# The last stage of layer 0 and the first of layer 1 made one in a two-layer attention kernel over a graph

## The chip, the cores and the metric

The kernel runs on one core of a Trainium2 chip. The time is the device time of one execution, in microseconds (us). The kernel before took 3869.91 us, the median of three runs (3863.47, 3869.91, 3873.05). Its profiled execution took 3871.49 us, with a span of 3869.6 us from the first to the last instruction.

## The reference

There are 3125 nodes with 64 features, and 100,000 edges from `src` to `dst`. A first part (`_L0_gnn_ref`) sends messages along the edges, sums them by node and runs three residual blocks; a layernorm follows. The part that matters here is two attention convolutions one after the other, each with two heads of 64:

```python
q = (x @ wq + bq).reshape(n, H, C)
k = (x @ wk + bk).reshape(n, H, C)
v = (x @ wv + bv).reshape(n, H, C)
alpha = jnp.einsum('ehc,ehc->eh', q[dst], k[src]) / jnp.sqrt(C)
amax = jax.ops.segment_max(alpha, dst, num_segments=n)
ex = jnp.exp(alpha - amax[dst])
a = ex / (denom[dst] + 1e-16)                 # denom: segment_sum(ex, dst)
out = jax.ops.segment_sum(a[:, :, None] * v[src], dst, num_segments=n)
return out.mean(axis=1) + x @ ws + bs
```

`x` of the second convolution is the result of the first. The sum of both and the residual goes through a last layernorm.

## The kernel before

The kernel computes the attention densely. A table of 3125 sources by 3136 targets holds how many edges each pair has; its logarithm is added to the scores, so that pairs without an edge vanish in the exponential. Sources are cut into NT = 25 tiles of 125, targets into CH = 7 chunks of D = 448. A score tile is 125 sources by 2 heads by 448 targets, in float32.

The first two thirds of the span (to about 2660 us) count the edges and do the first part of the model. The change does not touch them. Then come the two attention layers, `l` = 0 and 1. Each begins with projections: for each chunk a K and a Q matmul (L1101), which VectorE (DVE) and ScalarE (ACT) copy out (L874, L589), then V for 25 source tiles (L1106, copied with its bias at L879). Then come eight stages, `c` = 0 to 7. Stage `c` does two things at once:

- the scores of chunk `c`: TensorE (PE) multiplies (`scores`, L1121), DVE adds the logarithms (`score`, L898) and keeps a running maximum (`running`, L910);
- the weighted sums of chunk `c` - 1: GpSimd (POOL) subtracts the maximum of each target (L445), ACT takes the exponential (`exps`, L602), PE multiplies with V (`weighted`, L1144) and with ones for the denominators (L1153).

Stage 0 has only scores, stage 7 only weighted sums. In stage 7 DVE has no scores and takes 15 of the 25 subtractions (`by_vector`, L925). A stage ends when the maximum is known: PE transposes it (`move_max`, L1127), DVE reduces it (L916), PE spreads it over all partitions (`spread_max`, L1133), ACT copies it to `max_of_targets` (`spread`, L597). Only then can POOL begin on that chunk.

After the weighted sums of a chunk the denominators are copied (`copy_sums`), spread (L1159), copied again (`copy_spread`, L612) and inverted by DVE (`invert`, L931); POOL multiplies (`normalize`, L438) and PE projects (`project`, L1167 and L1168 in layer 0). ACT's `next_h` (L616) writes that chunk of layer 1's input. This happens one stage later, in the middle of it, for chunks 0 to 5; for chunk 6 it stands at the end of the layer, and layer 1's projections begin behind it.

Each engine runs its own list of instructions in the written order, and waits on semaphores. A matmul that writes a bank of the accumulation memory (`PS`) waits until the bank has been copied out. Scores alternate between banks 0, 1 and banks 2, 3; sums and denominators hold banks 4 and 5, the running maximum 6 and 7.

Of the kernel before, what the change touches and what calls it, by code (L numbers as in the profile page):

```python
# [7 lines left out]
F = 64  # L8
R = 16
P = 125  # L10
NT = N // P
# [11 lines left out]
CH = 7  # L23
LOADS = 2 * 7 + 2
BLK = 4
MW = 112
# [9 lines left out]
PP = PART + LEAD  # L36
INVERT = 11
# [3 lines left out]
assert SLOTS == NT + LEAD  # L41
# [20 lines left out]
def build(nc, x, src, dst, edge_attr, W_att, W_i, b_i, W_j, b_j, W_v, b_v, rd_W, rd_b, rr_W, rr_b, gate,  # L62
# [17 lines left out]
    with ctx:  # L80
# [153 lines left out]
        def by_vector(c, i):  # L234

            return c == CH - 1 and i % QN in (1, 3, 4)

        shifts = {}
        for v in range(2):
            n = 0  # L240
            for l in range(2):
                for c in range(CH):
                    for i in range(NT):
                        n += by_vector(c, i) == v
                        if by_vector(c, i) == v:
                            shifts[l, c, i] = n
# [6 lines left out]
        part_bank = 2 * (PP % 2)  # L253

        def slot_of(i):

            return (i + (i >= PP)) % 2
# [114 lines left out]
        def _(pool):  # L372
# [61 lines left out]
            for l in range(2):  # L434
                def normalize(c):
                    pool.wait_ge(sem("sums_out"), 2 * (l * CH + c + 1))
                    pool.wait_ge(sem("sums_inverted"), 2 * (l * CH + c + 1))
                    nc.gpsimd.tensor_tensor(AOn, AOn, DN, ALU.mult).then_inc(sem("normalized"), 1)  # L438

                for c in range(CH):  # L440
                    pool.wait_ge(sem("max_spread"), l * CH + c + 1)
                    for i in range(NT):
                        if not by_vector(c, i):
                            t = Ts[:, (l * ATT + c * NT + i) % SLOTS]
                            nc.gpsimd.tensor_tensor(t, t, MB, ALU.subtract).then_inc(sem("shifted"), 1)  # L445
                        if c and i == INVERT + 3:
                            normalize(c - 1)
                normalize(CH - 1)
# [3 lines left out]
        def _(act):  # L452
# [131 lines left out]
            for l in range(2):  # L584

                act.wait_ge(sem("bias_scaled"), 1)
                for c in range(CH):
                    act.wait_ge(sem("qk_in_psum"), 2 * (CH * l + c) + 2)
                    nc.scalar.activation(qT[:, c * D:(c + 1) * D], qk_bank(2 * c + 1), ACT.Identity, scale=0.125, bias=BC[:, 12 + l:13 + l]  # L589
                                         ).then_inc(sem("q_copied"), 1)  # L590
# [628 lines left out]
```

## Time and profile before

| | us |
|---|---|
| median of three runs | 3869.91 |
| profiled execution | 3871.49 |
| its span | 3869.6 |
| maximum of layer 0's chunk 6 spread (stage 7 can begin) | 3242.69 |
| layer 0's last projection begins | 3291.06 |
| first K and Q matmul of layer 1 | 3295.22 |
| first V matmul of layer 1 | 3316.29 |
| first scores of layer 1 | 3327.87 |
| maximum of layer 1's chunk 0 spread | 3388.84 |

Times are us from the start of the span. The two moments at which a maximum is spread are the start of ACT's copy plus its duration: 3241.77 + 0.92 and 3387.92 + 0.92. Between them lies the stretch that the change rewrites, 146.15 us. In rows of a timeline the first number is the start, the second the duration; several like instructions are merged, with "xN" their count. A float32 matmul shows as two records. PEclk is the granted TensorE clock as a share of 2.4 GHz: 1.00 is 2.4 GHz, 0.50 is 1.2 GHz.

### The profile page before, as it was taken

The page shows a single profiled execution, that of the slowest core. Times are in us where ns is not written, and L with a number is a line of the kernel's source. Part 1 is how long each engine was busy: PE and PEld are TensorE (multiplying, and loading weights), DVE is VectorE, ACT ScalarE, POOL GpSimd, SP SyncE. Part 2 cuts the span into 40 slices and gives each one's busy share as a digit, 9 for nine tenths or more (in the row PEclk, how much of TensorE's full clock was granted, in tenths as well). Part 3 has the DMA queues.
Part 4 walks back from the last instruction along what each step waited for, and adds up shares of the span by engine and source line. Part 5 has one row for each costly group of instructions (what it writes and reads, how often), then busy time and mean ns, then how long its engine had stood idle before and what let it go on. Part 6 is the DMA issues. An engine that isn't in the chain of part 4 may idle for free.

```text
span 3869.6 us, 56741 instructions
## 1 busy us (share of the span) xinstructions
PE 3063.6 (79%) x18659; PEld 1701.0 (44%) x18659; DVE 2706.2 (70%) x8606; ACT 669.4 (17%) x868; POOL 2811.3 (73%) x1917
## 2 busy tenths in 40 slices
PE   4787778777777877787778777876788888799996
PEld 3555555555555555555555555543222222322222
DVE  4666666666666666666666666656888888678786
ACT  2000000000000000000000000014343444043343
POOL 3588888888888888888888888872576776088684
PEclk7988898889889988988898889888799999699998
DMA  8411111111111111111111111113544452223330
GB/s 310 152 13 13 12 13 13 12 13 13 13 12 13 13 13 12 13 13 13 12 13 13 13 13 13 13 7 71 162 140 128 134 145 71 58 77 87 76 77 9
DMA packets 244257, 194.37 MB, mean 50 GB/s; under 512 B 146300, under 2 KB 224981, under 8 KB 244181
## 3 DMA queue, kind: packets, MB, share of 16 engines
q1 hardware_dynamic: 86035, 159.92, 13.9%
q0 software_dynamic: 137984, 26.19, 11.9%
q10 hardware_dynamic: 20162, 7.27, 0.9%
q8 instruction: 46, 0.75, 0.1%
q14 instruction: 30, 0.25, 0.0%
HBM read 112.79 MB, written 80.42 MB: 50 GB/s over the span
## 4 chain that ended last, share of the span: by engine, by line
DMA 28%; PE 20%; issue 19%; POOL 19%; DVE 9%; ACT 2%; SPq 2%; POOLq 1%; DVEq 0%; ACTq 0%
DMA edge_counts<-small 27%; POOL nodes_and_gaps L397 10%; POOL edge_counts L406 8%; PE PS L1121 7%; PE PS L1144 6%; PE PS L1153 3%; DVE counts_and_logs L886 2%; DVE scores L898 2%; DVE PS L910 2%; SPq L329 2%; DVE scores L925 1%; PE PS L1101 1%; PE PS L1133 1%; DMA edge_counts<-counts_and_logs 1%; PE PS L1127 0%
## 5 line engine op out<-in xcount | busy, mean ns | idle before, releaser
L1037 PE MATMUL PS<-scores 128*128 128x320 bf16 x11760 | 1839.8, 321 | 537.5 <-DVE scores L765 537.5
L1037 PEld LDWEIGHTS PS<-scores 128*128 128x128 bf16 x11760 | 1222.7, 105 | 1166.6 <-DVE scores L765 546.7
L406 POOL DMA_INDIRECT edge_counts<-small x752 | 1208.2, 1607 | 264.8 <-issue 264.8
L397 POOL DMA_INDIRECT nodes_and_gaps<-xj_rows,small x784 | 800.1, 1021 | 289.7 <-issue 129.2
L445 POOL TENSOR_TENSOR scores<-scores,max_of_targets 125x896 f32<-125x896 f32 x320 | 730.0, 2321 | 382.4 <-ACT max_of_targets L597 382.4
L726 DVE SCALAR_TENSOR_TENSOR scores<-PS,small,scores 128x256 bf16<-128x256 f32 x784 | 332.8, 480 | 666.6 <-PE PS L1017 666.5
L765 DVE TENSOR_SCALAR scores<-scores,small 128x192 bf16<-128x192 bf16 x3920 | 745.2, 296 | 3.5
L898 DVE TENSOR_TENSOR scores<-PS,counts_and_logs 125x896 f32<-125x896 f32 x350 | 377.5, 1082 | 146.7 <-PE PS L1153 61.1
L1121 PE MATMUL PS<-q_features,k_features 64*125 64x448 f32 x1400 | 383.6, 632 | 108.5 <-DVE scores L898 104.9
L602 ACT ACTIVATE scores<-scores 125x896 f32<-125x896 f32 x350 | 328.4, 948 | 360.2 <-POOL scores L445 346.6
L1144 PE MATMUL PS<-scores,v_nodes 125*64 125x448 f32 x1400 | 352.2, 591 | 20.3 <-ACT scores L602 20.3
L910 DVE TENSOR_TENSOR PS<-PS,scores 125x896 f32<-125x896 f32 x322 | 350.5, 1089 | 0.0
L739 DVE TENSOR_SCALAR scores<-scores,small 128x632 bf16<-128x632 f16 x784 | 281.9, 419 | 0.0
L1121 PEld LDWEIGHTS PS<-q_features,k_features 64*125 64x125 f32 x1400 | 113.4, 196 | 376.0 <-DVE scores L898 272.9
L521 ACT ACTIVATE scores<-nodes_and_gaps 128x512 bf16<-128x512 f32 x98 | 61.7, 630 | 1134.7 <-DVE nodes_and_gaps L748 1134.7
L516 ACT ACTIVATE scores<-PS 128x128 f32<-128x128 f32 x98 | 27.1, 277 | 1091.0 <-PE PS L1024 1091.0
L1153 PE MATMUL PS<-scores,dense_weights 125*32 125x448 f32 x1400 | 184.3, 575 | 0.0
L1144 PEld LDWEIGHTS PS<-scores,v_nodes 125*64 125x64 f32 x1400 | 74.1, 139 | 250.5 <-issue 149.9
L748 DVE TENSOR_TENSOR nodes_and_gaps<-nodes_and_gaps,PS 128x512 f32<-128x512 f32 x98 | 67.3, 687 | 114.6 <-DMA nodes_and_gaps<-xj_rows,small 114.2
L1016 PE MATMUL PS<-identity_scaled,keys 128*128 128x128 f16 x784 | 109.3, 220 | 15.0 <-ACT q_features L479 7.8
L1017 PE MATMUL PS<-identity,keys 128*128 128x128 f16 x784 | 109.4, 220 | 0.0
L886 DVE SCALAR_TENSOR_TENSOR counts_and_logs<-counts_and_logs 125x2240 f32<-125x2240 f32 x35 | 106.9, 3054 | 0.0
(162 smaller groups left out, 1714.9 us busy)
## 6 DMA issues: line engine op xcount, KB each, us to landing
counts_and_logs<-edge_counts SPq DMA_DIRECT2D x70, 980.0 KB
edge_counts<-counts_and_logs SPq DMA_DIRECT2D x50, 766.0 KB
edge_counts<-counts_and_logs SPq DMA_DIRECT2D x35, 980.0 KB
nodes_and_gaps<-xj_rows,small POOLq DMA_INDIRECT x784, 2.5
edge_counts<-small POOLq DMA_INDIRECT x752
counts_and_logs<-edge_counts SPq DMA_DIRECT2D x70, 113.8 KB
scores<-in_edge_attr_dram ACTq DMA_DIRECT2D x95, 48.0 KB
edge_counts<-counts_and_logs SPq DMA_DIRECT2D x35, 113.8 KB
```

The lines of the kernel that those rows point to most:

```text
L397: pool.indirect_dma_start(gx[u][:, s * F:(s + 1) * F], None, xj_dram, bass.IndirectOffsetOnAxis(ap=dcur[u][:, s:s + 1], axis=0)).then_inc( ...
L406: pool.indirect_dma_start(cnt_dram, bass.IndirectOffsetOnAxis(ap=index[:, s:s + 1], axis=0), value[:, s:s + 1], None, compute_op=ALU.add). ...
L445: nc.gpsimd.tensor_tensor(t, t, MB, ALU.subtract).then_inc(sem("shifted"), 1)
L602: nc.scalar.activation(t, t, ACT.Exp).then_inc(sem("weighed"), 1)
L726: nc.vector.scalar_tensor_tensor(ranked[:, s, :], PS[:, 5, 2 * EP * pair:2 * EP * pair + 2 * EP], keyc[:, s:s + 1], lowh[:, EP * (1 - e):E ...
L765: nc.vector.tensor_scalar(spread[:, s, :, k, :], pieces[:, :, s * F:(s + 1) * F], hi_is[:, k, s:s + 1], None, ALU.mult).then_inc(sem("tile ...
L898: nc.vector.tensor_tensor(Ts[:, n % SLOTS], score_slot[slot_of(i)], C5[k % CBUFS][:, i % QN].unsqueeze(1).to_broadcast([P, HEADS, D]), ALU ...
L910: nc.vector.tensor_tensor(RM if i == NT - 1 else RP, RP, Ts[:, n % SLOTS], ALU.max).then_inc(sem("max_run"), 1)
L1037: ins = nc.tensor.matmul(PS[:, b, 0:HI * F], onehot[:, s, b * P:b * P + 128], spread[:, s, i].rearrange("p h f -> p (h f)"), start=first a ...
L1121: ins = nc.tensor.matmul(score_slot[slot_of(i)][:, h, :], kT[q, i * P:(i + 1) * P], qT[q, c * D:(c + 1) * D], start=True, stop=True)
L1144: nc.tensor.matmul(AO[F * h:F * h + F, :], V[:, i, h, :], Ts[:, n % SLOTS, h, :], start=i == 0, stop=i == NT - 1, skip_group_check=True)
L1153: ins = nc.tensor.matmul(DEN[32 * g:32 * g + 32, :], ones, Ts[:, (n - i + e) % SLOTS, h, :], start=e < 2, stop=e >= NT - 2, skip_group_che ...
```

## The change

The stages are numbered `g` = 0 to 14 through both layers. Stage 7 of layer 0 and stage 0 of layer 1 become one, `g` = JOIN = 7, written out in a function of its own on PE, and layer 1's projections are spread over it:

- While the weighted sums of layer 0's chunk 6 run, PE does K and Q of layer 1 for chunk 0 to 4 behind weighted tile 0 to 4, projects chunk 5 of layer 0 behind tile 5 (before: behind tile 16), and does K and Q of chunk 5 behind tile 7.
- From weighted tile 8 on, a score tile of layer 1 stands behind each weighted tile (JLEAD = -8), 17 of them by the last weighted tile. Then come scores 17 to 20 with V of layer 1 between them, the projection of chunk 6, K and Q of chunk 6, and scores 21 to 24.
- All 25 subtractions of that stage go to POOL; `by_vector` holds only for the last stage of layer 1.
- V is copied out by ACT instead of DVE (an activation can't add a row of biases), so each V matmul is followed by a matmul that contracts over one row and adds the bias (`next_v`).
- Divisions of chunk 5 stand at the start of the stage on DVE, and POOL normalizes chunk 5 behind its third subtraction.

```diff
+LAST = 2 * CH - 1
+JOIN = CH
+JLEAD = -8
+JPP = 21
+JPART = 5
+EARLY = 17
-        def by_vector(c, i):
-            return c == CH - 1 and i % QN in (1, 3, 4)
+        def by_vector(g, i):
+            return g == LAST and i % QN in (1, 3, 4)
...
+                    if g == JOIN - 1 and i == 2 or projects(g + 1) is not None and i == INVERT + 3:
+                        normalize(g - 1)
+                if g == JOIN - 1:
+                    normalize(g)
...
+            def copy_v(b):
+                n = min(4, NT - 4 * b)
+                act.wait_ge(sem("v_in_psum"), 7 + b + 1)
+                nc.scalar.activation(V[:, 4 * b:4 * b + n].rearrange("p t h c -> p t (h c)"),
+                                     PS[0:P, 4 + b % 2, 0:n * 128].rearrange("p (t c) -> p t c", t=n), ACT.Copy).then_inc(sem("v_copied"), 1)
...
+                    if g == JOIN:
+                        if 1 <= i <= CH - 2:
+                            copy_q(1, i - 1, PS[:, 2 * ((i - 1) % 2) + 1, 0:D])
+                        if i == JPART + 1:
+                            next_h(CH - 2)
+                        if i == JPART + 3:
+                            copy_q(1, CH - 2, PS[:, 3, 0:D])
+                        if i == JPART + 5:
+                            begin_max(g)
...
+                if g == JOIN:
+                    for part in range(2):
+                        invert(g - 2, part)
+                    for c in range(CH - 1):
+                        copy_k(1, c, PS[:, 2 * (1 if c == CH - 2 else c % 2), 0:D])
+                    for i in range(EARLY + 2):
+                        score_and_run(g, i)
+                    for part in range(2):
+                        invert(g - 1, part)
+                    for i in range(EARLY + 2, JPP):
+                        score_and_run(g, i)
+                    copy_k(1, CH - 1, PS[:, 2, 0:D])
...
+            def next_qk(c, r):
+                pe.wait_ge(sem("attended"), c + 1)
+                for j, w in enumerate((wk_(1), wq_(1))):
+                    nc.tensor.matmul(PS[:, 2 * r + j, 0:D], w, h_(1, c * D, D), start=True, stop=True).then_inc(sem("qk_in_psum"), 1)
+
+            def next_v(b):
+                if b >= 2:
+                    pe.wait_ge(sem("v_copied"), 7 + b - 1)
+                for t in range(4 * b, min(4 * b + 4, NT)):
+                    to = PS[0:P, 4 + b % 2, t % 4 * 128:(t % 4 + 1) * 128]
+                    nc.tensor.matmul(to, h_(1, t * P, P), wv_(1), start=True, stop=False)
+                    ins = nc.tensor.matmul(to, ones[0:1, 0:1].to_broadcast([1, P]), BR[0:1, 128:256], start=False, stop=True)
+                ins.then_inc(sem("v_in_psum"), 1)
...
+            def join(g):
+
+                pe.wait_ge(sem("scored"), g * NT)
+                for i in range(NT):
+                    weighted(g - 1, i)
+                    if i < CH - 2:
+                        if i >= 2:
+                            pe.wait_ge(sem("k_copied"), CH + i - 1)
+                            pe.wait_ge(sem("q_copied"), CH + i - 1)
+                        next_qk(i, i % 2)
+                    if i == JPART:
+                        pe.wait_ge(sem("k_copied"), CH + CH - 3)
+                        project(g - 2)
+                    if i == JPART + 2:
+                        pe.wait_ge(sem("q_copied"), CH + CH - 3)
+                        next_qk(CH - 2, 1)
+                    if i + JLEAD >= 0:
+                        if i + JLEAD == 0:
+                            pe.wait_ge(sem("k_copied"), CH + CH - 1)
+                            pe.wait_ge(sem("q_copied"), CH + CH - 1)
+                        scores(g, i + JLEAD)
+                scores(g, EARLY)
+                spread_sums(g - 1)
+                scores(g, EARLY + 1)
+                pe.wait_ge(sem("spread_copied"), g)
+                next_v(0)
+                next_v(1)
+                scores(g, EARLY + 2)
+                next_v(2)
+                next_v(3)
+                scores(g, EARLY + 3)
+                next_v(4)
+                pe.wait_ge(sem("scored"), g * NT + JPP - 1)
+                project(g - 1)
+                next_qk(CH - 1, 1)
...
+                scores(g, JPP)
+                scores(g, JPP + 1)
+                next_v(5)
+                scores(g, JPP + 2)
+                next_v(6)
+                scores(g, JPP + 3)
+                move_max(g)
+                spread_max(g)
```

PE at the start of stage 7, in the list of the kernel before. L1133 spreads the maximum of chunk 6, L1159 the denominators of chunk 5; L1144 are weighted sums and L1153 denominators.

```order
L1127 MATMUL PS<-identity,running_max 112x125 x8
L1144 MATMUL PS<-scores,v_nodes 64x448 x2
L1153 MATMUL PS<-scores,dense_weights 32x448 x2
L1133 MATMUL PS<-identity,small 125x112 x8
L1159 MATMUL PS<-dense_weights 128x448
L1144 MATMUL PS<-scores,v_nodes 64x448 x4
L1153 MATMUL PS<-scores,dense_weights 32x448 x4
```

The same place in the changed kernel, whose line numbers are its own: L1209 are weighted sums, L1218 denominators, and L1165 is K and Q of layer 1.

```order
L1224 MATMUL PS<-dense_weights 128x448
L1209 MATMUL PS<-scores,v_nodes 64x448 x2
L1165 MATMUL PS<-h_features,layer_weights 128x448 x2
L1209 MATMUL PS<-scores,v_nodes 64x448 x2
L1218 MATMUL PS<-scores,dense_weights 32x448 x4
L1165 MATMUL PS<-h_features,layer_weights 128x448 x2
L1209 MATMUL PS<-scores,v_nodes 64x448 x2
L1165 MATMUL PS<-h_features,layer_weights 128x448 x2
```

K and Q moved from behind the layer to between the first weighted tiles.

PE from the end of stage 7 to the end of layer 1's stage 0, before: L1167 and L1168 project chunk 6, L1101 is K and Q, L1106 is V, L1121 are scores.

```order
L1144 MATMUL PS<-scores,v_nodes 64x448 x2
L1153 MATMUL PS<-scores,dense_weights 32x448 x2
L1159 MATMUL PS<-dense_weights 128x448
L1167 MATMUL PS<-dense_weights 64x448
L1168 MATMUL PS<-h_features,layer_weights 64x448
L1101 MATMUL PS<-h_features,layer_weights 128x448 x14
L1106 MATMUL PS<-layer_weights,h_features 125x128 x25
L1121 MATMUL PS<-q_features,k_features 125x448 x50
L1127 MATMUL PS<-identity,running_max 112x125 x8
```

In the changed kernel, from the last weighted tile: L1186 are scores, L1172 is V and L1173 its bias.

```order
L1186 MATMUL PS<-q_features,k_features 125x448 x2
L1209 MATMUL PS<-scores,v_nodes 64x448 x2
L1218 MATMUL PS<-scores,dense_weights 32x448 x2
L1186 MATMUL PS<-q_features,k_features 125x448 x4
L1224 MATMUL PS<-dense_weights 128x448
L1186 MATMUL PS<-q_features,k_features 125x448 x2
L1172 MATMUL PS<-layer_weights,h_features 125x128
L1173 MATMUL PS<-bias_rows,dense_weights 125x128
```

Further on, where V's tile 19 is followed by the projection of chunk 6 (L1230, L1231):

```order
L1172 MATMUL PS<-layer_weights,h_features 125x128
L1173 MATMUL PS<-bias_rows,dense_weights 125x128
L1230 MATMUL PS<-dense_weights 64x448
L1231 MATMUL PS<-h_features,layer_weights 64x448
L1165 MATMUL PS<-h_features,layer_weights 128x448 x2
L1186 MATMUL PS<-q_features,k_features 125x448 x4
L1172 MATMUL PS<-layer_weights,h_features 125x128
L1173 MATMUL PS<-bias_rows,dense_weights 125x128
```

V now stands behind score tile 18, in pairs with its bias, and the projection of chunk 6 behind score tile 20, where before all 50 score matmuls stood behind both.

## Rows read from the trace of the kernel before

**Rows 1.** The page, busy time of each engine in the span

```profile
PE 3063.6 (79%) x18659; PEld 1701.0 (44%) x18659; DVE 2706.2 (70%) x8606; ACT 669.4 (17%) x868; POOL 2811.3 (73%) x1917
```

**Rows 2.** Windows (us, busy us of PE, PEld, DVE, ACT, POOL; clock; DMA), stages

```profile
3242.00:3289.00 47.00, 38.92 (x208) 9.02 (x206) 38.69 (x19) 26.13 (x31) 30.91 (x11) 0.93 0.00 1
3289.00:3328.00 39.00, 35.51 (x84) 20.82 (x84) 10.06 (x16) 5.06 (x8) 1.13 (x1) 0.52 0.00 0
3328.00:3388.00 60.00, 38.05 (x126) 14.58 (x128) 50.66 (x51) 1.00 (x2) 0.00 (x0) 0.76 0.36 94
3388.00:3456.00 68.00, 63.27 (x326) 18.02 (x326) 51.67 (x51) 26.90 (x30) 51.35 (x25) 0.97 0.32 83
```

**Rows 3.** Timeline (start, us, engine, line, what), ACT

```profile
3241.77 0.92 ACT L597 ACTIVATE max_of_targets<-PS 125x896 f32<-125x896 f32 x1 [0.85 <-PE PS L1133]
...
3294.54 0.63 ACT L616 ACTIVATE h_features<-PS,bias_columns 64x448 f32<-64x448 f32 x1 [7.80 <-PE PS L1168]
...
3387.92 0.92 ACT L597 ACTIVATE max_of_targets<-PS 125x896 f32<-125x896 f32 x1 [56.01 <-PE PS L1133]
```

**Rows 4.** Timeline, PE, weighted sums at the start of stage 7

```profile
3246.78 3.25 PE L1144 MATMUL PS<-scores,v_nodes 125*64 125x448 f32 x8 [4.27 <-ACT scores L602]
3249.96 1.72 PE L1153 MATMUL PS<-scores,dense_weights 125*32 125x448 f32 x8
3251.61 2.22 PE L1144 MATMUL PS<-scores,v_nodes 125*64 125x448 f32 x8
```

**Rows 5.** Windows of PE alone (us, busy us; clock; DMA), K, Q, V of both layers

```profile
3295.00:3316.40 21.40, 21.18 (x29) 0.50 0.00 0
3316.40:3327.20 10.80, 10.76 (x51) 0.50 0.00 0
2667.30:2678.00 10.70, 10.67 (x29) 1.00 0.66 156
2678.00:2684.20 6.20, 6.09 (x51) 1.00 1.05 253
```

**Rows 6.** Timeline, PE, projections of chunk 5 and chunk 6

```profile
3271.16 0.92 PE L1167 MATMUL PS<-dense_weights 128*64 128x448 f32 x2
...
3272.90 0.97 PE L1144 MATMUL PS<-scores,v_nodes 125*64 125x448 f32 x4
...
3291.06 1.75 PE L1167 MATMUL PS<-dense_weights 128*64 128x448 f32 x2 [4.90 <-POOL dense_weights L438]
```

**Rows 7.** The page, the exponentials

```profile
L602 ACT ACTIVATE scores<-scores 125x896 f32<-125x896 f32 x350 | 328.4, 948 | 360.2 <-POOL scores L445 346.6
```

**Rows 8.** Timeline, POOL

```profile
3289.88 1.13 POOL L438 TENSOR_TENSOR dense_weights<-dense_weights 128x448 f32<-128x448 f32 x1 [13.65 <-DVE dense_weights L931]
3388.92 51.35 POOL L445 TENSOR_TENSOR scores<-scores,max_of_targets 125x896 f32<-125x896 f32 x25 [97.91 <-ACT max_of_targets L597]
```

**Rows 9.** Timeline, PE, a pair of tiles in layer 1's stage 1

```profile
3400.85 1.02 PE L1121 MATMUL PS<-q_features,k_features 64*125 64x448 f32 x4
3401.80 0.97 PE L1144 MATMUL PS<-scores,v_nodes 125*64 125x448 f32 x4
...
3404.56 0.96 PE L1153 MATMUL PS<-scores,dense_weights 125*32 125x448 f32 x8
3405.45 1.02 PE L1121 MATMUL PS<-q_features,k_features 64*125 64x448 f32 x4
```

**Rows 10.** Timeline, DVE: two divisions, and the last tiles of layer 1's stage 0

```profile
3286.78 2.96 DVE L931 RECIPROCAL dense_weights<-dense_weights 128x224 f32<-128x224 f32 x2 [7.58 <-ACT dense_weights L612]
...
3377.43 1.08 DVE L898 TENSOR_TENSOR scores<-PS,counts_and_logs 125x896 f32<-125x896 f32 x1
3378.43 1.09 DVE L910 TENSOR_TENSOR PS<-PS,scores 125x896 f32<-125x896 f32 x1
3379.62 1.09 DVE L910 TENSOR_TENSOR running_max<-PS,scores 125x896 f32<-125x896 f32 x1
```

**Rows 11.** Windows of all engines, inside layer 1's stage 0

```profile
3336.00:3338.00 2.00, 1.02 (x8) 0.29 (x4) 2.00 (x3) 0.00 (x0) 0.00 (x0) 1.00 0.00 0
3342.00:3344.00 2.00, 1.86 (x6) 0.50 (x4) 2.00 (x3) 0.00 (x0) 0.00 (x0) 0.50 0.29 61
```

More of the change, by code:

```diff
@@ L962, in _ @@
+            for part in range(2):
+                invert(LAST, part)
+            outputs(CH - 1)
             dve.wait_ge(sem("attended"), 2 * CH)
@@ new lines, in scores @@
+            def scores(g, i):
+                n = g * NT + i
+                pause = pause_of(g)
+                if n >= 2:
+                    pe.wait_ge(sem("scored"), n if i == pause else n - 2 if i == pause + 1 else n - 1)
+                if i == pause + 1 and projects(g) is not None:
+                    pe.wait_ge(sem("attended"), g - 1)
+                c = g % CH
+                for h in range(HEADS):
+                    q = slice(F * h, F * h + F)
+                    ins = nc.tensor.matmul(score_slot[slot_of(g, i)][:, h, :], kT[q, i * P:(i + 1) * P], qT[q, c * D:(c + 1) * D], start=True, stop=True)
+                ins.then_inc(sem("scores_in_psum"), 1)
@@ new lines, in weighted @@
+            def weighted(g, i):
+                n = g * NT + i
+                pe.wait_ge(sem("weighed"), n + 1)
+                if i == 0 and g:
+                    pe.wait_ge(sem("sums_out"), 2 * g)
+                for h in range(HEADS):
+                    nc.tensor.matmul(AO[F * h:F * h + F, :], V[:, i, h, :], Ts[:, n % SLOTS, h, :],
+                                     start=i == 0, stop=i == NT - 1, skip_group_check=True)
+                if i % 2 == 0 and i < NT - 1:
+                    return
+                if i == 1 and g:
+                    pe.wait_ge(sem("spread_copied"), g)
+                for e in range(i - i % 2, i + 1):
+                    for h in range(HEADS):
+                        q = 2 * (e % 2) + h
+                        ins = nc.tensor.matmul(DEN[32 * q:32 * q + 32, :], ones, Ts[:, (n - i + e) % SLOTS, h, :],
+                                               start=e < 2, stop=e >= NT - 2, skip_group_check=True)
+                ins.then_inc(sem("weighted_sums"), 1 + i % 2)
@@ new lines, in _ @@
+            for g in range(2 * CH + 1):
+                if g == JOIN:
+                    join(g)
+                    continue
+                for i in range(LEAD):
+                    if g <= LAST:
+                        scores(g, i)
+                for i in range(NT):
+                    if g:
+                        weighted(g - 1, i)
+                    if projects(g) is not None and i == PART:
+                        pe.wait_ge(sem("scored"), min(2 * ATT, g * NT + PP - 1))
+                        project(g - 2)
+                    if g <= LAST and i + LEAD < NT:
+                        scores(g, i + LEAD)
+                    if g <= LAST and i == NT - 2:
+                        move_max(g)
+                if g <= LAST:
+                    spread_max(g)
+                if g:
+                    spread_sums(g - 1)
```

456 lines of the change are left out of this document (210 added, 246 removed).

## The prediction, on record before the changed kernel ran

> **What bounds the kernel now.** The page's busy shares come first, and they mislead: PE 79%, POOL 73%, DVE 70% are means over parts with different limits [rows 1]. So I read windows by stage next. The change rewrites one stretch, from the moment when layer 0's last maximum is spread, 3241.77 + 0.92 = 3242.69, to the moment when layer 1's first one is, 3387.92 + 0.92 = 3388.84 [rows 3]. That is 146.15 us, and nothing ahead of it or behind it changes its list. The stretch has three parts, each with another limit [rows 2]. Stage 7 of layer 0 (47 us): PE is 38.92 us busy and DVE 38.69. Projections (39 us): PE is busy for 35.51 us while DVE has 10, ACT 5, POOL 1, and the clock is 0.52. Stage 0 of layer 1 (60 us): DVE is busy for 50.66 us, POOL idle, PE at 38.05 with a clock of 0.76. The reader is to see that in each part other engines stand still, so laying the parts over each other can gain much, until one engine has the sum of the work. A mixed stage, for comparison, takes 68 us with PE at 63.27 and a clock of 0.97 [rows 2]: there PE is the limit.
>
> **Prices.** At the full clock (2.4 GHz) a score tile costs PE 0.95 us (3400.85 to 3401.80), the denominators of two tiles 0.89 (3404.56 to 3405.45), and two tiles in all 4.60 (3400.85 to 3405.45), so a weighted tile (4.60 - 1.90 - 0.89) / 2 = 0.90 [rows 9]. At 1.2 GHz two weighted tiles cost 3249.96 - 3246.78 = 3.18, so 1.6 each, and denominators 1.65 [rows 4]; a score tile 1.86 [rows 11]. K and Q of a chunk: 21.4 / 7 = 3.0 at the half clock, 10.7 / 7 = 1.53 at the full one; V: 10.8 / 25 = 0.43 or 6.2 / 25 = 0.25 a tile [rows 5]. A projection of layer 0: 3272.90 - 3271.16 = 1.74 full, 3294.54 - 3291.06 = 3.48 half [rows 3, 6]. POOL: 51.35 / 25 = 2.05 a subtraction beside DVE's scores, 1.13 a normalization [rows 8]. DVE: 1.0 from one operation to the next, so 2.0 a score tile [rows 10]. ACT: 0.95 an exponential [rows 7], 0.63 a copy of 448 columns [rows 3]; with a semaphore on each side I count 0.8 for a copy on which PE waits.
>
> The bias matmul that follows each V matmul has no row. It streams the same 128 columns; its price lies between nothing (if it runs beside V's, on other rows of the array) and that of a V matmul. I take the upper end, since columns seem to set the price: a K or Q matmul has 448 and costs 10.7 / 14 = 0.76, of which 128 / 448 is 0.22, near V's 0.25 [rows 5]. So four V tiles cost 2.0 us at full clock (between 1.0 and 2.0) and 3.45 at half.
>
> **The clock decides the sum.** K, Q and V of layer 1 kept PE busy for 31.94 of 32.2 us at 0.50 and never rose; the same instructions in layer 0 began at 1.00 and stayed there [rows 5]. These matmuls use 64 of the array's 128 rows. Weighted tiles, which use nearly all rows and columns, bring the clock back: at the start of stage 7 they cost the half-clock price until about 3251.6, five us after the first [rows 4]. Scores alone swing between 1.00, with PE busy half of the time, and 0.50 at 1.86 of 2.00 [rows 11]. So sparse matmuls seem to count for less.
>
> The Trainium skill, "TensorE: Matmul & The Clock Gate", section "Part 1: The HAM clock gate", says that the gate follows how busy PE has lately been, and that sustained matmuls release it. By that rule the joined stage, where PE hardly pauses, would run at 2.4 GHz to the end; it is the first rival below. The stretch of 32 us at 0.50 [rows 5] does not agree with busy time alone as the measure.
>
> **The sum, with t = 0 at 3242.69.**
>
> 1. K, Q and the first nine weighted tiles. PE's first weighted tile starts as before, at t = 3246.78 - 3242.69 = 4.1. Weighted tile 0, K and Q of chunk 0, tile 1 and the first denominators at half clock: 1.6 + 3.0 + 1.6 + 1.65 = 7.9, t = 12.0. Then the clock is full: seven weighted tiles 6.3, three denominators 2.7, five K and Q 7.7, the projection of chunk 5 1.7, together 18.4; and a wait for the last Q copy, 0.8: t = 31.2. POOL has exponential 8 ready by 9 x 2.05 + 1.13 + 0.95 = 20.5, so losing DVE's help in subtracting costs nothing: the 15 subtractions moved are hidden behind PE. The two divisions of chunk 5 (2.96, [rows 10]) are done before POOL's third subtraction.
> 2. Scores 0 to 16 among weighted tiles 9 to 24: 17 x 0.95 + 16 x 0.90 + 8.5 x 0.89 = 38.1, t = 69.3. DVE needs 2.0 a tile against PE's 2.3, POOL ends at 25 x 2.05 + 1.13 = 52.4. PE is the limit.
> 3. The tail. Score 17, the spread of denominators, score 18: 0.95 + 0.9 + 0.95, t = 72.1. ACT's copies end meanwhile. V 0 and 1: 4.0, t = 76.1. Score 19 and V 2: 3.0, t = 79.1. Here I let the clock fall, since half of each V pair contracts over 64 rows and the other half over one. V 3 3.45, score 20 1.86, V 4 3.45, t = 87.8. Divisions (2.96) and normalization (1.13) of chunk 6 start at about 74 on DVE, behind score 18, and end by 79: not late. Projection 3.5, copy 0.8, K and Q 3.0, copy 0.8: t = 95.9. Scores 21, 22, V 5, score 23, V 6, score 24: 4 x 1.86 + 3.45 + 0.86 = 11.8, t = 107.7. DVE: last score and two maxima 3.2: t = 110.9.
> 4. From the last maximum to its spread: 3388.84 - (3379.62 + 1.09) = 8.1 [rows 3, 10]. t = 119.0.
>
> So 119 in place of 146, a gain of 27. Against the profiled execution, 3871.5 - 27 = 3844.5; that execution was 1.6 above the median of 3869.9, so for the median 3843.
>
> Transfers: the count tables of layer 1 are loaded three buffers deep. In stage 0 each score tile takes 2.0, here never less, and the windows show the DMA at 0.36 of its time [rows 2], so none is late. What was hidden before and is not any more: V's copies on ACT, seven of about 0.7; V runs two banks ahead, so they cost nothing while ACT has no exponentials left.
>
> **The rivals.**
>
> A. The clock stays full through the tail. Then part 3 is: t = 79.1 after V 2, V 3 2.0, score 20 0.95, V 4 2.0 (84.0), projection 1.7, copy 0.8, K and Q 1.5, copy 0.8 (88.8), score 21 0.95; then DVE with four tiles and one more maximum, 9.1, is the limit (98.9), and 8.1: 107. Gain 39, time 3831. For it: V and K and Q kept 1.00 in layer 0 [rows 5]. Against it: no bias matmuls stood between them there. If these are also hidden, the tail is 5 shorter: 3826. This is also what the page's rule on the clock would give.
>
> B. The start stays slow as well. If weighted tiles mixed with K and Q don't raise the clock before the first scores: 4.1 + 9 x 1.6 + 4 x 1.65 + 6 x 3.0 + 3.5 + 0.8 = 47.4 in place of 31.2, 16 later, t = 135, gain 11: 3859. For it: K and Q take half of PE's time there and never raised the clock themselves. Against it: a weighted tile with denominators, 3.3 us of full rows, stands between every second pair. With the full tail instead, the gain is 23, near my forecast.
>
> C. Slower: the clock never rises in the joined stage, because K and Q hold it down at the start and scores (64 rows a head) behind them. Then part 2 costs 17 x 1.86 + 16 x 1.6 + 8.5 x 1.65 = 71.2 in place of 38.1, 33 more; part 1 16 more; the rest of the tail up to V 2 another 7: 119 + 56 = 175, which is 29 over 146: 3899. It decides from about 27 us of added PE time, so only if half of part 2 or more stays at 1.2 GHz. Against it: every mixed stage of scores and weighted sums runs at 0.97 [rows 2].
>
> D. The overlap fails elsewhere: ACT runs exponentials and Q copies in one list, each Q copy waiting for PE, so a cycle PE to ACT to POOL could hold PE in part 1 by a copy and an exponential, 1.7, in each of six steps: 10 more. Gain 17, time 3853.
>
> **Chances.** Forecast (gain 20 to 33) 0.42; A (over 33) 0.36; B and D (5 to 20) 0.18; within 0.3% 0.01; C 0.03. About 0.3%, 12 us, is what a measurement of this kernel can tell from no change. The range takes in A with its hidden bias matmuls and all of B and leaves out C: low 3825, high 3859. B's gain of 11 lies just within the bound of no change. So faster 0.92, same 0.05 (B's worst part among it), slower 0.03.
>
> **What would show it.** First scores of layer 1 about 31 us after the last spread of layer 0 (B: 47). Scores 0 to 16 at 2.3 us a tile with a clock of 1.00. PE's clock falling during V (A: staying at 1.00), and the time from score 17 to the next spread of the maximum near 50 us (A: 38). POOL's 25 subtractions ending near t = 53, ahead of PE. The whole from spread to spread 119 us. Wrong would be: PE idle in part 1 behind ACT, DVE waiting for loads, or any change of length in stages behind the join.

## The result: 0.997 of the time before, a third of the forecast gain

| | us | against before |
|---|---|---|
| before, 20 runs | 3869.39 median | |
| changed, 20 runs | 3859.68 median (3849.03 to 3876.37) | ratio 0.997, 95% interval 0.9956 to 0.9985 |
| forecast | 3843, range 3825 to 3859 | |
| stretch from spread to spread, before | 146.15 | |
| the same, changed | 3378.60 - 3240.25 = 138.35 | 7.8 shorter (forecast 27) |

The kernel is faster by about 10 us where 27 were forecast, just outside the range. The changed kernel's profiled execution has a span of 3856.4 us, 13.2 less than before, and only 7.8 of it lies in the rewritten stretch. The other 5.4 lie where both kernels have the same lists: 2.4 ahead of it and 3.0 behind. Single executions differ by that much there, so I judge each part by its place in the trace and the whole by the times.

The two ends of the stretch on ACT in the changed kernel (start, duration, engine, line; compare [rows 3]):

```profile
3239.33 0.92 ACT L612 ACTIVATE max_of_targets<-PS 125x896 f32<-125x896 f32 x1 [0.85 <-PE PS L1198]
...
3377.68 0.92 ACT L612 ACTIVATE max_of_targets<-PS 125x896 f32<-125x896 f32 x1 [12.12 <-PE PS L1198]
```

With t = 0 at 3240.25, PE's first weighted tile starts at t = 3.2 (forecast 4.1), the first scores of layer 1 come at t = 37.5 (forecast 31.2), score 16 ends at 75.9 (69.3), the last maximum at 130.2 (110.9), its spread at 138.4 (119.0). PE's timeline at the start (compare [rows 4] and [rows 6]):

```profile
3243.48 1.72 PE L1209 MATMUL PS<-scores,v_nodes 125*64 125x448 f32 x4 [3.42 <-issue]
3245.13 3.35 PE L1165 MATMUL PS<-h_features,layer_weights 64*128 64x448 f32 x4
3248.42 1.76 PE L1209 MATMUL PS<-scores,v_nodes 125*64 125x448 f32 x4
3250.11 1.72 PE L1218 MATMUL PS<-scores,dense_weights 125*32 125x448 f32 x8
...
3269.77 0.96 PE L1230 MATMUL PS<-dense_weights 128*64 128x448 f32 x2
...
3277.71 1.02 PE L1186 MATMUL PS<-q_features,k_features 64*125 64x448 f32 x4
```

A pair of K and Q takes 3.3 us here, the price at 1.2 GHz, and everything up to 3264 runs at that clock. The windows of PE alone (us, busy us, granted clock, DMA share, GB/s) show where the clock rises and falls:

```profile
3248.00:3252.00 4.00, 4.00 (x14) 0.50 0.00 0
...
3260.00:3264.00 4.00, 4.00 (x14) 0.50 0.02 4
3264.00:3268.00 4.00, 4.00 (x14) 0.99 0.00 0
...
3277.00:3315.00 38.00, 38.00 (x200) 1.00 0.28 69
...
3320.00:3322.00 2.00, 2.00 (x11) 1.00 0.00 0
3322.00:3328.00 6.00, 6.00 (x19) 0.51 0.00 0
3328.00:3341.00 13.00, 13.00 (x38) 0.50 0.34 86
```

PE is busy without a gap from 3244 to 3264 and from 3320 to 3348; the clock is 0.50 through the first and from 3322 on in the second. In the tail the V matmuls with their biases stand at two prices:

```profile
3319.98 0.48 PE L1173 MATMUL PS<-bias_rows,dense_weights 1*125 1x128 f32 x2
3320.39 0.48 PE L1172 MATMUL PS<-layer_weights,h_features 64*125 64x128 f32 x2
...
3332.79 0.78 PE L1173 MATMUL PS<-bias_rows,dense_weights 1*125 1x128 f32 x2
3333.50 0.79 PE L1172 MATMUL PS<-layer_weights,h_features 64*125 64x128 f32 x2
3334.22 0.78 PE L1173 MATMUL PS<-bias_rows,dense_weights 1*125 1x128 f32 x2
```

From start to start that is 0.41 us at 2.4 GHz and 0.71 at 1.2, for either kind. V alone had cost 0.25 and 0.43 [rows 5]. VectorE shows what the tail waits for (compare [rows 10]):

```profile
3329.73 1.09 DVE L935 TENSOR_TENSOR scores<-PS,counts_and_logs 125x896 f32<-125x896 f32 x1 [4.27 <-PE PS L1186]
3330.74 1.09 DVE L946 TENSOR_TENSOR PS<-PS,scores 125x896 f32<-125x896 f32 x1
3342.64 1.09 DVE L935 TENSOR_TENSOR scores<-PS,counts_and_logs 125x896 f32<-125x896 f32 x1 [10.81 <-PE PS L1186]
```

It stands still for 10.81 us until PE has done eight V tiles and comes to score 20.

### The profile page after: what moved, and what is told of

Read it like the earlier page. It is cut to its first block, busy times and chain, and to the rows that moved or that the text cites. A ratio compares the mean times of both kernels' runs of the same rounds, so it can differ in the third digit from the quotient of the medians.

```text
span 3856.4 us, 56845 instructions
## 1 busy us (share of the span) xinstructions
PE 3084.1 (80%) x18709; PEld 1710.6 (44%) x18709; DVE 2670.8 (69%) x8584; ACT 672.0 (17%) x875; POOL 2830.8 (73%) x1932
## 4 chain that ended last, share of the span: by engine, by line
POOL 33%; issue 22%; PE 22%; DMA 11%; DVE 8%; ACT 2%; SPq 2%; POOLq 1%; DVEq 0%; ACTq 0%
POOL edge_counts L420 17%; POOL nodes_and_gaps L411 16%; DMA edge_counts<-small 10%; PE PS L1186 7%; PE PS L1209 6%; PE PS L1218 3%; DVE counts_and_logs L923 2%; SPq L343 2%; DVE PS L946 2%; DVE scores L935 1%; PE PS L1198 1%; DMA edge_counts<-counts_and_logs 1%; PE PS L1192 0%; PE PS L1090 0%; PE PS L1165 0%
## 5 line engine op out<-in xcount | busy, mean ns | idle before, releaser
L458 POOL TENSOR_TENSOR scores<-scores,max_of_targets 125x896 f32<-125x896 f32 x335 | 751.9, 2282 | 332.3 <-ACT max_of_targets L612 332.3
L1186 PE MATMUL PS<-q_features,k_features 64*125 64x448 f32 x1400 | 380.8, 627 | 89.0 <-DVE scores L935 85.7
L1209 PE MATMUL PS<-scores,v_nodes 125*64 125x448 f32 x1400 | 355.7, 593 | 21.0 <-ACT scores L617 17.4
L1186 PEld LDWEIGHTS PS<-q_features,k_features 64*125 64x125 f32 x1400 | 112.4, 194 | 347.5 <-DVE scores L935 244.1
L1209 PEld LDWEIGHTS PS<-scores,v_nodes 125*64 125x64 f32 x1400 | 73.2, 139 | 252.8 <-issue 152.1
L1218 PE MATMUL PS<-scores,dense_weights 125*32 125x448 f32 x1400 | 181.4, 569 | 0.0
L1082 PE MATMUL PS<-scores 128*128 128x512 f32 x196 | 106.5, 625 | 0.0
```

The costliest lines, as they stand in the source:

```text
L1186: ins = nc.tensor.matmul(score_slot[slot_of(g, i)][:, h, :], kT[q, i * P:(i + 1) * P], qT[q, c * D:(c + 1) * D], start=True, stop=True)
L1209: nc.tensor.matmul(AO[F * h:F * h + F, :], V[:, i, h, :], Ts[:, n % SLOTS, h, :], start=i == 0, stop=i == NT - 1, skip_group_check=True)
L1218: ins = nc.tensor.matmul(DEN[32 * q:32 * q + 32, :], ones, Ts[:, (n - i + e) % SLOTS, h, :], start=e < 2, stop=e >= NT - 2, skip_group_che ...
```

## The experiments

The theory after the result: the missing 19 us are 6.3 at the start and 12.7 in the tail, both on PE. In the tail each bias matmul makes its V matmul dearer, since the two use different rows of the array, and pulls the clock down; at the start the clock fell in PE's wait and rose late. The rivals: V is dear wherever it stands among scores; accumulating right behind a matmul into the same place is what costs; the clock has another reason; the start is held by ACT's chain. Each run was compared with runs of the kernel before on the same chip. A kernel with the four V matmuls of a group first and their four biases behind them was planned too; there is no measurement of it.

### VectorE adds the bias again

```diff
-                    nc.tensor.matmul(to, h_(1, t * P, P), wv_(1), start=True, stop=False)
-                    ins = nc.tensor.matmul(to, ones[0:1, 0:1].to_broadcast([1, P]), BR[0:1, 128:256], start=False, stop=True)
+                    ins = nc.tensor.matmul(to, h_(1, t * P, P), wv_(1), start=True, stop=True)
...
+                    add_v(0)
+                    add_v(1)
                     for part in range(2):
                         invert(g - 1, part)
-                    for i in range(EARLY + 2, JPP):
-                        score_and_run(g, i)
+                    score_and_run(g, EARLY + 2)
+                    add_v(2)
+                    add_v(3)
+                    score_and_run(g, EARLY + 3)
+                    add_v(4)
...
```

> The changed kernel with V of layer 1 copied and biased by VectorE again, so the 25 one-row bias matmuls are gone; all else as changed. In the changed kernel V and bias cost 0.71 us a matmul at 1.2 GHz (1.43 a tile) where V alone cost 0.43. Theory 1 (the bias matmuls cost both their own time and a dearer V, by switching between them): V falls to 0.43 a tile at half clock or 0.25 at full, the tail from score 17 to the last maximum (54 us now) falls by 17 to 25 us, to 30 to 37, and the kernel is 17 to 25 us faster than the changed one. Rival (V for rows 64 to 127 is dear wherever it stands among scores): V stays at 0.71 and the tail falls by 18 or less at the same clock, and by no more if the clock falls all the same. If the bias matmuls also pulled the clock down, it stays at 1.00 through V and the tail is near 30.

Measured: 3849.03 us, ratio 0.9932 (0.9914 to 0.995). The stretch is 112.6 us, 26 less than changed. Its tail, from the end of score 16 to the last maximum, fell from 54.3 to 35.0, within the band for theory 1. The time missed its band: it is 11 us under the changed kernel's median, where 17 to 25 were expected (15 if each is compared with its own runs of before, 24 against 10). Of the 26 us in the trace, 6.5 are the start, which was short in this one execution. V costs 0.22 a tile here while the clock is 1.00 (from start to start in single records, which the view merges):

```profile
3334.33 1.58 PE L1184 MATMUL PS<-layer_weights,h_features 64*125 64x128 f32 x13
...
3338.72 1.68 PE L1184 MATMUL PS<-layer_weights,h_features 64*125 64x128 f32 x13 [1.73 <-DVE v_nodes L981]
...
3344.73 1.65 PE L1184 MATMUL PS<-layer_weights,h_features 64*125 64x128 f32 x8 [3.25 <-DVE v_nodes L981]
```

The rival, V dear among scores, is out. The rows also show the mend's own price: PE waits 1.73 and 3.25 us for VectorE, which has copies, divisions and scores in one list, and behind the second wait the clock is 0.52. The part at the start took 31.0 us in this execution with an unchanged list; more on that under the filled wait.

### The bias over 128 rows

```diff
-                    ins = nc.tensor.matmul(to, ones[0:1, 0:1].to_broadcast([1, P]), BR[0:1, 128:256], start=False, stop=True)
+                    ins = nc.tensor.matmul(to, share[:, 0:1].to_broadcast([128, P]), BR[:, 128:256], start=False, stop=True)
```

`share` is a column of 1/128.

> The changed kernel with the bias matmul contracting over all 128 rows (weights 1/128, the bias row in every partition) instead of over one row; same count, columns and order. Theory on the clock (matmuls on few rows count for little in what holds the clock up, so V with one-row bias let it fall 3.5 us after V began): the clock stays at 1.00 through V, V and bias cost 0.41 us each throughout instead of 0.71, the tail is 10 to 16 us shorter. Rival (the clock falls by how densely PE is fed, or for another reason): the clock falls at the same place, the tail is the same within 2 us. The price of a matmul at a given clock should not change if the switch between row sets sets it.

Measured: 3842.81 us, ratio 0.9921 (0.9901 to 0.9941); the stretch is 122.4 us, 16 less than changed, all of it in the tail (10 to 16 were expected). The clock, in windows of PE alone over V and the projection:

```profile
3321.00:3327.00 6.00, 6.00 (x32) 1.00 0.06 6
3327.00:3335.00 8.00, 8.00 (x41) 1.00 0.52 136
```

and the price at this clock:

```profile
3333.25 0.48 PE L1174 MATMUL PS<-layer_weights,h_features 64*125 64x128 f32 x2
3333.66 0.48 PE L1175 MATMUL PS<-bias_rows,share_column 128*125 128x128 f32 x2
```

Same count, same columns, same order, same price of 0.41, but the clock holds. So how many rows a matmul uses does bear on the clock: with one-row biases it fell during V in all three executions on record (the changed kernel, the one with the start filled, the one with a bias for four tiles), with 64 or 128 rows it stayed at 1.00 there. PE's being busy is not enough. The price at full clock is untouched, so it has another cause than the clock.

### The bias over V's own rows

```diff
-                    ins = nc.tensor.matmul(to, ones[0:1, 0:1].to_broadcast([1, P]), BR[0:1, 128:256], start=False, stop=True)
+                    ins = nc.tensor.matmul(to, share[F:128, 0:1].to_broadcast([F, P]), BR[F:128, 128:256], start=False, stop=True)
```

Here `share` is 1/64, on rows 64 to 127, which V uses too.

> The changed kernel with the bias matmul contracting over rows 64 to 127, the same rows of the array as V's (weights 1/64, bias in every partition); count, columns and order as changed. V and bias cost 0.41 us a matmul at 2.4 GHz and 0.71 at 1.2 there, with one row and with 128 rows alike. Theory R (the excess over V alone, 0.25 and 0.43, comes from going from one set of rows to another): with the same rows each costs 0.25 or 0.43. Rival A (it comes from accumulating into the place that the matmul just before wrote): still 0.41 or 0.71.

Measured: 3832.01 us in a single execution; the same kernel, timed again under "The best version", took 3830.23. Each matmul costs 0.22 us from start to start:

```profile
3316.05 0.38 PE L1175 MATMUL PS<-bias_rows,share_column 64*125 64x128 f32 x2
3316.27 0.38 PE L1174 MATMUL PS<-layer_weights,h_features 64*125 64x128 f32 x2
3316.49 0.38 PE L1175 MATMUL PS<-bias_rows,share_column 64*125 64x128 f32 x2
```

The accumulation into the same 128 columns is the same as in the two kernels before, so rival A is out: the excess of 0.19 us a matmul at 2.4 GHz, and 0.28 (0.71 - 0.43) at 1.2, comes with the bias's rows.

Theory R as worded, that any change of rows costs this, goes too far. The two heads of a score tile stand on rows 0 to 63 and 64 to 127, one matmul after the other, and pay nothing for it. Two score tiles behind each other in the changed kernel, four matmuls of 448 columns in eight records, take 1.70 us from the first to what follows, and single records of the two heads start 0.007 us apart. Two matmuls of 448 columns that use the same 64 rows take 1.53 [rows 5]:

```profile
3315.34 1.77 PE L1186 MATMUL PS<-q_features,k_features 64*125 64x448 f32 x8
3317.04 1.02 PE L1224 MATMUL PS<-dense_weights 128*128 128x448 f32 x2
```

And in this kernel the first matmul of score 19 (L1188, rows 0 to 63) starts while V's last tile (L1174, rows 64 to 127) is still under way:

```profile
3318.45 0.27 PE L1174 MATMUL PS<-layer_weights,h_features 64*125 64x128 f32 x1
3318.46 0.64 PE L1188 MATMUL PS<-q_features,k_features 64*125 64x448 f32 x1
3318.56 0.27 PE L1174 MATMUL PS<-layer_weights,h_features 64*125 64x128 f32 x1
```

So another set of rows of the same size is free here, and overlaps. In both dear kernels the neighbours differ in the number of rows as well (64 and 1, 64 and 128). That this number is what counts is the reading that fits all these rows; no run changed it alone.

The clock is 1.00 through V:

```profile
3315.00:3320.00 5.00, 5.00 (x44) 1.00 0.00 0
3320.00:3326.00 6.00, 6.00 (x52) 1.00 0.31 81
```

The tail is 104.5 - 74.3 = 30.2 from the last weighted tile to the last maximum, where the changed kernel has 130.2 - 74.3 = 55.9.

Weight loads tell where part of the time goes. In this kernel each load begins while the matmul before still runs (start to start 0.22, load 0.29 for two records). In the kernel over 128 rows the loads take the same 0.29 but begin 0.41 apart:

```profile
3315.94 0.29 PEld L1175 LDWEIGHTS PS<-bias_rows,share_column 64*125 64x125 f32 x2
3316.16 0.29 PEld L1174 LDWEIGHTS PS<-layer_weights,h_features 64*125 64x125 f32 x2
```

```profile
3326.32 0.29 PEld L1175 LDWEIGHTS PS<-bias_rows,share_column 128*125 128x125 f32 x2
3326.73 0.29 PEld L1174 LDWEIGHTS PS<-layer_weights,h_features 64*125 64x125 f32 x2
```

The Trainium skill, "TensorE: Matmul & The Clock Gate", section "Part 3: Packing small matmuls — row/col tiling", says that a weight load overlaps matmuls in flight only when its row group differs. The same section of the Trainium skill also lets a load run ahead when it goes to the background weight buffer. The score tiles agree with the first sentence, since their heads use different rows and overlap. The V matmuls do not: loads for the same rows are hidden (0.22 us, which the background buffer would allow), and with one row against 64, two sets that share no row, they are not (0.41). Where they differ the measurement decides.

Of the 0.19 us, one exposed load explains about half: in the kernel over 128 rows the two load records of a matmul start 0.105 us apart. What the other 0.09 is, is not shown.

### One bias matmul for four tiles

```diff
+                nc.tensor.matmul(PS[0:P, 4 + b % 2, 0:n * 128].rearrange("p (t c) -> p t c", t=n), ones[0:1, 0:1].to_broadcast([1, P]),
+                                 BR[0:1, 128:256].unsqueeze(1).to_broadcast([1, n, 128]), start=True, stop=True)
...
-                    nc.tensor.matmul(to, h_(1, t * P, P), wv_(1), start=True, stop=False)
-                    ins = nc.tensor.matmul(to, ones[0:1, 0:1].to_broadcast([1, P]), BR[0:1, 128:256], start=False, stop=True)
+                    ins = nc.tensor.matmul(to, h_(1, t * P, P), wv_(1), start=False, stop=True, skip_group_check=True)
```

> The changed kernel with one one-row bias matmul over 512 columns for four V tiles, ahead of the four V matmuls, in place of one of 128 columns behind each. Same columns, 7 bias matmuls instead of 25, no V matmul directly behind the matmul on the same 128 columns but the first, and one change of rows per four tiles. Theory R and rival A both expect V near 0.25 at 2.4 GHz (0.43 at 1.2) and the bias at 512 / 448 x 0.76 = 0.87 (1.7): 1.9 us for four tiles at full clock instead of 3.3, 3.4 at half instead of 5.7. If V still costs 0.41 or 0.71, both are wrong and reading V's operands or writing that bank is slow here. The tail (54 us) becomes 38 to 43 us if the clock falls, about 32 if not.

Measured, in a single execution: the stretch is 130.4 us, the clock falls to 1.2 GHz in V's second group (t = 81.4), and from the last weighted tile to the last maximum it takes 122.3 - 74.1 = 48.2 (55.9 in the changed kernel). Counted from the end of score 16, as the expectation does, that is 46.5, outside its 38 to 43. From start to start a bias and its four V matmuls cost 1.05 + 1.07 = 2.1 us at full clock and 2.0 + 2.0 = 4.0 at half, where 1.9 and 3.4 were expected:

```profile
3358.14 1.12 PE L1171 MATMUL PS<-bias_rows,dense_weights 1*125 1x512 f32 x2
3359.18 1.14 PE L1175 MATMUL PS<-layer_weights,h_features 64*125 64x128 f32 x8
3360.25 1.30 PE L1171 MATMUL PS<-bias_rows,dense_weights 1*125 1x512 f32 x2
...
3366.96 2.06 PE L1175 MATMUL PS<-layer_weights,h_features 64*125 64x128 f32 x8
3368.96 2.06 PE L1171 MATMUL PS<-bias_rows,dense_weights 1*125 1x512 f32 x2
```

Its own time was 3891.46, 22 over before, though the stretch is 16 shorter than before's: the stretch begins at 3279.62 in this execution instead of 3242.69, in a part whose list is the same. A single time says nothing of a change of this size. The expectation left out the two changes of rows in each group. With them it comes out: 4 x 0.22 + 0.85 (512 columns) + 2 x 0.19 = 2.1 at full clock, 3.4 + 2 x 0.28 = 4.0 at half. Fewer changes of rows bring the price down, one-row matmuls still take the clock down.

### PE's wait at the start filled

```diff
                 pe.wait_ge(sem("scored"), g * NT)
+                for _ in range(4):
+                    nc.tensor.matmul(PS[:, 0, 0:D], ident[:, :], WL[:, 0:D], start=True, stop=True)
                 for i in range(NT):
                     weighted(g - 1, i)
```

> The changed kernel with four dense matmuls (128 rows, 128 x 448) added in PE's idle time at the start of the joined stage, about 3 us, whose result nobody reads. Theory (part 1 was 6 us longer than forecast only since the clock fell in the idle 3.4 us and rose 19 us later instead of 8): the clock stays at 1.00 and first scores come at t = 28 to 31 instead of 37.5, the stage is 6 to 9 us shorter. Rival (part 1 is held by ScalarE's chain of exponentials and copies, or the clock falls anyway with K and Q): first scores not before t = 35.

Measured: 3851.69 us, ratio 0.9944 (0.9927 to 0.996). First scores at t = 27.7 instead of 37.5, and the clock stays at 1.00 until V (t = 71.4):

```profile
3258.30 3.17 PE L1244 MATMUL PS<-layer_weights,identity 128*128 128x448 f32 x8
3261.84 0.97 PE L1209 MATMUL PS<-scores,v_nodes 125*64 125x448 f32 x4 [0.37 <-ACT scores L617]
3262.74 1.77 PE L1165 MATMUL PS<-h_features,layer_weights 64*128 64x448 f32 x4
```

The rest of the stretch is 3 us longer than in the changed kernel (131.6 - 27.7 = 103.9, there 138.4 - 37.5 = 100.9): once it fell in V the clock stayed down, where in the changed kernel it was back at 1.00 from t = 119.4 to 122.8. So the stretch is 6.7 shorter, not 9.8. The chain through ACT is no limit: PE waits for it 0.37 us ahead of the first weighted tile and 0.79 behind the projection.

The same list without fillers gave first scores at 37.5, 31.0, 37.3, 37.5, 37.3 and 37.5 us in six executions of five kernels. Once, in the kernel where VectorE adds the bias, the clock rose at t = 11.3, near the 12 of the forecast; five times it rose at 23.4 to 23.9. Windows of that kernel's PE on either side of the rise, with t = 0 at 3262.21:

```profile
3266.81:3273.21 6.40, 6.40 (x17) 0.50 0.00 0
3274.21:3285.21 11.00, 11.00 (x46) 1.00 0.01 1
```

Why it rose early that once is not shown.

### Both mends, and more fillers

> The changed kernel with both mends: V's bias added by VectorE in its copy (no bias matmuls), and four dense matmuls into PE's idle time at the start of the joined stage. If the two act apart, the stretch from spread to spread is 27.7 (first scores) + 36.8 (scores 0 to 16) + 36.6 + 8.1 = 109 us against 138.3 in the changed kernel and 146.2 before: 29 less than changed, 37 less than before, so about 0.990 of before. If VectorE becomes the limit earlier, since it now copies V too, little less than the 112.6 that the first mend gave alone.

Measured: 3833.05 us, ratio 0.9912 (0.9897 to 0.9928), stretch 109.6 (expected 109). The parts add.

The next adds fillers in the tail of that kernel, written as `keep(n, bank)`: n matmuls of 128 rows and 384 columns into a bank that is free. Two of the places:

```diff
...
                 scores(g, EARLY + 3)
+                pe.wait_ge(sem("scored"), g * NT + JPP - 1)
+                keep(3, 3)
                 next_v(4)
-                pe.wait_ge(sem("scored"), g * NT + JPP - 1)
                 project(g - 1)
+                keep(1, 3)
                 next_qk(CH - 1, 1)
...
```

> As the kernel with both mends, and dense matmuls (128 rows, 128 x 384, result unread) in the places of the tail where PE waits: two behind score 19, three behind score 20, one behind the projection of chunk 6, one behind K and Q of chunk 6, six behind score 24, two ahead of the spread of the maximum. Theory on the clock (it falls in PE's waits of 1.7 and 3.3 us for VectorE and stays down through projection, K, Q and scores): it stays at 1.00, the projection costs 1.7 instead of 3.5, K and Q 1.6 instead of 3.1, scores 21 and 22 1.8 instead of 3.2, the spread 2.0 instead of 3.7: 5 to 8 us less than with both mends, 101 to 104 us. Rival (the fillers stand in the way, since VectorE and not PE is the limit): within 2 us of it or longer.

Measured: 3825.7 us, ratio 0.9902 (0.9885 to 0.9918), stretch 105.7: 3.9 less, not the 5 to 8 expected. The fillers held the clock in part. It fell for 3.5 us at t = 77.9, right behind PE's wait of 1.65 us for VectorE, and was back for projection, K and Q, which cost 1.8 and 1.7 us:

```profile
3312.00:3316.40 4.40, 3.82 (x6) 0.61 0.62 161
3316.40:3324.00 7.60, 7.60 (x29) 1.00 0.22 54
```

Against that, the three fillers of the wait ran mostly at 1.2 GHz and stood in the way: V's fifth group began at t = 81.5 instead of 79.2. So theory and rival each hold for a part. Of the 3.9, 1.3 come from the last step, 6.8 us instead of 8.1.

### The best version

Own rows for the bias and the filler at the start:

> The changed kernel with the bias matmuls on V's own rows and four dense matmuls in PE's idle time at the start of the joined stage. The same rows alone made the tail 30.2 us (54.3 in the changed kernel), the fillers alone the first scores come at 27.7 (37.5). If the parts add: 27.7 + 36.8 + 30.2 + 8.1 = 103 us from spread to spread, against 138.3 changed and 146.2 before, and a time about 0.989 of before. If the part at the start was only a matter of luck in that one execution, first scores at 31 to 37.5 again and 107 to 113 us.

Measured: 3825.31 us, ratio 0.9886 (0.9869 to 0.9902). First scores at 27.7, last maximum at 94.7, stretch 102.8: as expected to 0.2 us. Here the clock falls only at t = 92.4, just ahead of the last maximum. With `keep(6, 0)` behind score 24 and `keep(2, 0)` ahead of the spread:

> As the last, with six dense matmuls behind score 24 and two ahead of the spread of the maximum. In every kernel so far without them the step from the last maximum to its spread took 8.1 us at 1.2 GHz, with them 6.7. Theory: the clock stays up, 6.7 or less, 101 to 102 us from spread to spread, a gain of 1 to 2 us that the times alone can't show. Rival: nothing, or a delay where a filler stands in the way of the transposes.

Measured: 3818.06 us, ratio 0.9873 (0.9858 to 0.9888). The stretch is 100.3 us (101 to 102 were expected); the step from the last maximum to its spread took 5.6 us instead of 8.1:

```profile
3331.26 1.09 DVE L948 TENSOR_TENSOR running_max<-PS,scores 125x896 f32<-125x896 f32 x1
```

```profile
3337.00 0.92 ACT L613 ACTIVATE max_of_targets<-PS 125x896 f32<-125x896 f32 x1 [10.07 <-PE PS L1200]
```

The intervals of the last two overlap, so the trace and not the time shows the end fillers' 2.5 us.

> The kernel with the bias matmuls on V's own rows again, now timed: one edit to the changed kernel. If the 26 us that its stretch is shorter than in the changed kernel (112.6 against 138.3) are real time, the median is 22 to 30 us under the changed kernel's 3859.7, 0.991 of before. Its profile is a second look at part 1, whose list is unchanged: first scores at 31.0 or 37.3 to 37.5 as in the five executions so far, and V and bias 0.22 us each if the clock holds.

Measured: 3830.23 us, ratio 0.9902 (0.9886 to 0.9918), stretch 112.6 again, first scores at 37.5. One edit to the changed kernel, the rows of the bias, is worth 29 us against its median of 3859.68, where the trace gave 26. Compared each with its own runs of before, it is 35.0 against 9.7, so 25.

## Why the prediction was wrong, step by step

The mechanism of the change was right: parts that had stood behind each other overlap, and PE is the limit. The cost on PE was set too small. From spread to spread, by the four steps of the forecast:

| step | forecast | changed | best version |
|---|---|---|---|
| 1. to the first scores | 31.2 | 37.5 | 27.7 |
| 2. scores 0 to 16 | 38.1 | 38.5 | 38.5 |
| 3. tail, to the last maximum | 41.6 | 54.3 | 28.5 |
| 4. to its spread | 8.1 | 8.1 | 5.6 |
| sum | 119.0 | 138.4 | 100.3 |

The step that failed is the price in step 3: "So four V tiles cost 2.0 us at full clock (between 1.0 and 2.0) and 3.45 at half." They cost 3.2 and 5.7. I took the price of V alone as an upper end for V with a bias matmul, and it was none, since that row shows matmuls that all use one set of rows. In the price of rows 5 the weight load is hidden behind the matmul before; going to and fro between 64 rows and one exposes it. The seven groups took 30.3 us where the forecast had 17.2, and the difference of 13 covers the tail's excess of 12.7. About 11 of the 13 is the price itself, at the clock that I had assumed (3 x 3.3 + 3 x 5.7 + 1.4 = 28.4); the rest is the clock, earlier down for V 1 and V 2 and back up for V 5. The runs bear this out from both sides: V's own rows remove the excess at once, and with 128 rows, where the clock stays up, a matmul still costs 0.41.

The clock in the tail fell behind V 0 (t = 81.8), two groups earlier in the list than I let it, though 2.7 us later in time. That it would fall, against rival A, was right, and the reason given, few rows, is what the run over 128 rows shows. A clock that stays up through V, as in rival A, came with the biases over 64 or 128 rows, not in this kernel.

Step 1: the clock rose at t = 24 instead of 12. Rival B had priced a rise after the first scores, 47.4; the truth lay between. Giving 8 us of half clock as the likeliest was a choice from rows of dense weighted tiles [rows 4], while here every second piece is K and Q. With fillers the step is 27.7, below the forecast. Two small misses all but cancel in it: the first tile started 0.9 us earlier than forecast, and a pair of K and Q between weighted tiles costs 1.70 at full clock (3266.28 to 3267.98), not the 1.53 of K and Q in a row. The 0.8 us that I gave to the last Q copy fell elsewhere, on an exponential; that the sizes agree is luck.

Steps 2 and 4, the prices of scores, weighted tiles, projections and copies, and the hidden 15 subtractions (POOL ended at 52.3 us, forecast 52.4) were as forecast. Rivals C and D fell: with the clock up, scores among weighted tiles hold it at 1.00, and once the first exponential is there ACT holds PE in step 1 for 0.8 us in all.

## What to carry to other kernels

A price from a row holds for the neighbours that the row had. Where a change puts a new matmul between two old ones, ask whether it uses the same rows of the array as they do, or as many of the others: a matmul over one row or all 128 beside matmuls over 64 cost 0.19 us here at every change, and both old and new got dearer, while two sets of 64 rows cost nothing. Work moved from a part where an engine idles into one where it is the limit must be priced there, and on PE the clock belongs to the price: a wait of 3.4 us ahead of sparse matmuls cost 3 to 10 us in the traces, and four dummy matmuls in it gave them back.

## What the runs showed of the hardware

- Float32 matmuls of 128 columns on the same 64 rows: 0.22 us each at 2.4 GHz. Alternating with matmuls over one row or over 128: 0.41 each (over one row 0.71 at 1.2 GHz).
- Matmuls on rows 0 to 63 and on rows 64 to 127 overlap: the two heads of a score tile start 0.007 us apart.
- 26 us of PE without a gap at 0.50 (3322 to 3348), most of it V with one-row biases, and 1.00 over the same list with 128-row or 64-row biases. V and bias on rows 64 to 127 alone held 1.00 in the last case; K, Q and V of layer 1 on the same rows never raised it from 0.50 before the change, and those of layer 0 kept 1.00 [rows 5]. In these rows holding it took less than raising it.
- The part ahead of the stretch, whose list was the same in all kernels, ended between 3234.94 and 3279.62 us. Single times of this kernel can't tell 10 us.
